# Transposing seven of ten probability blocks of each attention head with VectorE and DMA in place of TensorE

## The reference, cut to what matters

```python
q = jnp.einsum('bpd,hde->bphe', x, W_Q) + b_Q        # k, v likewise
scores = jnp.einsum('bqhe,bkhe->bhqk', q, k) / ATTN_SCALE
scores = jnp.where(causal, scores, IGNORE)
attn = jax.nn.softmax(scores, axis=-1)
z = jnp.einsum('bkhe,bhqk->bqhe', v, attn)
out = jnp.einsum('bqhe,hed->bqd', z, W_O) + b_O
```

## Time and profile before

| | |
|---|---|
| median of 3 runs | 533.88 us |
| the profiled execution | 534.24 us |
| its span | 532.4 us |
| TensorE (PE) busy | 514.5 us, 97% |
| weight loads (PEld) | 464.4 us, 87% |
| VectorE (DVE) | 385.2 us, 72% |
| ScalarE (ACT) | 292.8 us, 55% |
| GpSimd (POOL) | 191.9 us, 36% |
| mean granted TensorE clock | 0.989 of full |

### The profile page before, as it was taken

How to read it: one execution, slowest core, us unless ns; L and a number is a source line. 1 busy time by engine, 2 the same in 40 slices (tenths; PEclk the granted TensorE clock), 3 DMA queues, 4 the chain that set the end, 5 groups by cost and what they waited for, 6 DMA issues and landing times.

```text
span 532.4 us, 9326 instructions
## 1 busy us (share of the span) xinstructions
PE 514.5 (97%) x3302; PEld 464.4 (87%) x3302; DVE 385.2 (72%) x970; ACT 292.8 (55%) x688; POOL 191.9 (36%) x277
## 2 busy tenths in 40 slices
PE   8999999999999899999999999999999999999972
PEld 7888889898888789999999999999998999999861
DVE  2757876855555978768668668777777787667897
ACT  2446533564545565655656656566566565665552
POOL 2236142434656335214223223322512543222234
PEclk9999999999999999999999999999999999999995
DMA  9900000000000021000200200200200200000002
GB/s 281 356 6 1 1 0 1 2 1 1 2 0 1 0 81 46 36 1 1 80 1 1 81 2 1 79 2 2 80 0 2 80 2 0 2 1 0 2 2 79
DMA packets 8333, 17.52 MB, mean 33 GB/s; under 512 B 480, under 2 KB 6752, under 8 KB 7264
## 3 DMA queue, kind: packets, MB, share of 16 engines
q1 hardware_dynamic: 7200, 15.89, 8.7%
q10 hardware_dynamic: 1088, 1.05, 0.6%
HBM read 15.88 MB, written 1.05 MB: 32 GB/s over the span
## 4 chain that ended last, share of the span: by engine, by line
PE 86%; DVE 7%; ACT 2%; DMA 2%; issue 1%; POOL 1%; SPq 0%; DVEq 0%; ACTq 0%
PE bank L303 20%; PE bank L305 20%; PE bank L304 20%; PE bank L559 6%; PE bank L550 4%; PE bank L549 4%; PE bank L551 4%; PE bank L488 3%; PE bank L487 3%; DMA Wv_sb<-wv 2%; PE bank L498 1%; PE bank L500 1%; DVE XN L1021 1%; DVE SM L1291 1%; PE bank L354 1%
## 5 line engine op out<-in xcount | busy, mean ns | idle before, releaser
L797 ACT ACTIVATE PR<-SM,nmax 128x128 f32<-128x128 f32 (+3 forms) x128 | 71.9, 562 | 100.7 <-DVE nmax L1291 100.5
L1291 DVE CUSTOM_DVE_ANT_0 SM<-bank,causal 128x128 f32<-128x128 f32 (+3 forms) x128 | 60.7, 484 | 18.4 <-PE bank L551 18.3
L962 POOL TENSOR_TENSOR PR<-PR,rec 128x128 f32<-128x128 f32 x32 | 12.8, 400 | 140.2 <-DVE rec L1298 140.2
L1302 DVE TENSOR_TENSOR PT_lo<-bank,PT_hi 128x128 fp32r<-128x128 f32 (+3 forms) x128 | 59.3, 485 | 2.1 <-ACT PT_hi L802 0.3
L802 ACT CAST PT_hi<-bank 128x128 fp32r<-128x128 f32 (+3 forms) x128 | 50.0, 423 | 5.1 <-PE bank L559 4.3
L303 PE MATMUL bank<-XT_hi,W_hi 128*128 128x512 f32 x128 | 50.6, 395 | 0.2 <-DVE XT_lo L1029 0.2
L918 POOL TENSOR_TENSOR E_lo<-E,E_hi 128x512 fp32r<-128x512 f32 x24 | 31.0, 1297 | 54.6 <-ACT E_hi L721 47.6
L305 PE MATMUL bank<-XT_hi,W_lo 128*128 128x512 f32 x128 | 50.5, 395 | 0.0
L304 PE MATMUL bank<-XT_lo,W_hi 128*128 128x512 f32 x128 | 50.4, 394 | 0.0
L559 PE MATMUL bank<-ident,PR 128*128 128x128 f32 x320 | 46.2, 273 | 1.8 <-DVE PT_lo L1302 0.8
L549 PE MATMUL bank<-K_hi,Q_hi 128*128 128x256 f32 (+2 forms) x128 | 46.5, 364 | 0.0
(11 more groups left out here) (174 smaller groups left out, 1621.9 us busy)
## 6 DMA issues: line engine op xcount, KB each, us to landing
stage<-pack SPq DMA_DIRECT2D x8, 1027.0 KB, 4.9
X<-x SPq DMA_DIRECT2D x2, 512.0 KB, 8.8
wraw<-wupT SPq DMA_DIRECT2D x1, 1024.0 KB, 10.1
wraw<-wgateT SPq DMA_DIRECT2D x1, 1024.0 KB, 12.0
wraw<-wdownT SPq DMA_DIRECT2D x1, 1024.0 KB, 15.8
Wq_sb<-wq ACTq DMA_DIRECT2D x3, 256.0 KB, 5.3
Wk_sb<-wk SPq DMA_DIRECT2D x3, 256.0 KB, 4.7
Wv_sb<-wv SPq DMA_DIRECT2D x3, 256.0 KB, 8.4
```

Source lines behind the costliest of these rows:

```text
L797: act.activation(PR[:, c, 0:(c + 1) * P], SM[:, c % 2, 0:(c + 1) * P], ACT.Exp, bias=nmax1[:, c:c + 1], scale=-1.0, accum_out=sum1[:, c:c ...
L1291: dve.tensor_tensor_reduce(SM[:, c % 2, 0:n], bank[2 + c % 2][:, 0:n], causal[:, SEQ - n:SEQ], 1.0, HIGHEST, ALU.add, ALU.min, nmax1[:, c: ...
L1302: dve.tensor_tensor(PT_lo[w % 2][:, 0:c + 1, c * P:(c + 1) * P], bank[4 + c % 2][:, 0:(c + 1) * P].rearrange("p (j q) -> p j q", q=P), PT_ ...
```

## The change

For windows 1 to 25 only T0 and T1 stay on TensorE. T2 and T3 (seven blocks) go another way:

- DVE transposes row blocks 2 and 3 of PR, in SBUF, in blocks of 32x32 into `BT` (`U2` at the end of the window before, `U3` early in the head's window). What is left is to exchange the 32-partition strips.
- SyncE issues 12 DMAs, one for each pair of different strips: 32 partitions x 8 runs of 128 B, 32 KB each, from `BT` to `MV`. The four strips that stay in their partitions are copied by ACT (`D0` to `D3`, 32 partitions x 256 elements each).
- One window later ACT rounds MV to PT_hi (`C2`, `C3`), POOL (not DVE) writes PT_lo (`moved_low`), and PE does the product with V (`B0`) near the window's end, after S3.
- Output projections are spread, one part in each window, a head pair later; Z_hi and Z_lo exist twice.
- The refills of `stage` are issued by ACT, no longer by SyncE.
- The 256-column minimum is gone: row block 0 of the scores and the last key block of the product with V stream 128 columns, everywhere. With it go six memsets (four on POOL, two on DVE); two memsets of BT on POOL are new.
- Windows 27 to 31 keep their lists; 0, 1 and 26 have lists of transition.

The diff, cut to its core:

```diff
+QUAD = P // 4
+MOVES = 16 * 12
...
+        memb = ExitStack()
+        BT = [sb(f"BT{i}", [P, CT, 2, P], F32, memb) for i in range(2)]
+        MV = [sb(f"MV{i}", [P, CT, 2, P], F32, memb) for i in range(2)]
...
+        FIRST_MOVED, LAST_MOVED = 1, WINDOWS - 7
+        STEADY_PE = (steps("T0 T1 S0 O0 S1 Q0 S2 K1 S3 B0 V2"), steps("T0 T1 S0 Q0 S1 O0 S2 K1 S3 B0 V2"))
+        STEADY_ACT = (steps("W2 T0 T1 S0 C2 C3 S1 Q0 D0 D1 S2 D2 D3 K1 B0 S3"),
+                      steps("W2 T0 T1 S0 Q0 C2 C3 S1 D0 D1 S2 D2 D3 K1 B0 S3"))
+        STEADY_DVE = (steps("S0 W2 U3 T0 T1 O0 S1 Q0 S2 R0 K1 S3 B0 R1 U2"),
+                      steps("S0 W2 U3 T0 T1 S1 Q0 O0 S2 R0 K1 S3 B0 R1 U2"))
...
+            0: steps("T0 T1 S0 T2 T3 S1 Q0 S2 K1 A0 S3 V2"),
+            1: steps("T0 T1 S0 S1 Q0 S2 K1 S3 V2"),
+            WINDOWS - 6: steps("T0 T1 S0 O0 S1 T2 T3 Q0 S2 K1 B0 S3 V2 A0"),
+            WINDOWS - 5: EVEN_PE,
...
+        def by_dma(w):
+
+            return FIRST_MOVED <= w <= LAST_MOVED
+
+        def moved_windows(w):
+
+            return max(0, min(w, LAST_MOVED + 1) - FIRST_MOVED)
+
+        def turns(w):
+
+            return CT * w - 2 * moved_windows(w)
...
+            return (w - 3) // 2 if w % 2 else (w - 4) // 2, 1 - w % 2
...
-            for p in range(1, PAIRS):
-
-                sp.wait_ge(wb_dve, p)
-                sp.wait_ge(wb_pool, p)
-                sp.dma_start(stage[:], pack1[p]).then_inc(ld_pack, 16)
+            sp.wait_ge(bt_zero, 1)
+            for w in range(FIRST_MOVED, LAST_MOVED + 1):
+                sp.wait_ge(bt_done, 2 * moved_windows(w + 1))
+                if w >= FIRST_MOVED + 2:
+                    sp.wait_ge(mv_lo, 2 * moved_windows(w - 1))
+                for j in range(CT):
+                    for i in range(CT):
+                        if i == j:
+                            continue
+                        sp.dma_start(MV[w % 2][j * QUAD:(j + 1) * QUAD, :, :, i * QUAD:(i + 1) * QUAD],
+                                     BT[w % 2][i * QUAD:(i + 1) * QUAD, :, :, j * QUAD:(j + 1) * QUAD]
+                                     ).then_inc(moved[w % 2], 16)
...
-                n = max((c + 1) * P, 2 * P)
+                n = (c + 1) * P
...
-                pe.wait_ge(t_free, 4 * w + c + 1)
+                if w > 0 or c > 1:
+                    pe.wait_ge(t_free, turns(w) + c - 1)
...
-                pe.wait_ge(t_free, 4 * w + 6)
+                pe.wait_ge(t_free, turns(w + 1))
+                if by_dma(w):
+                    pe.wait_ge(mv_lo, 2 * moved_windows(w + 1))
                 pe.wait_ge(z_free, w + 1)
                 if h == 0:
                     pe.wait_ge(pj_lo, 6 * (g + 1))
-                if w == 1:
-                    pe.wait_ge(pt_zero, 1)
                 for j in range(CT):
-                    q0 = min(j * P, SEQ - 2 * P)
+                    q0 = j * P
...
+                    cols = slice(max(2 * r, j) * P, 2 * (r + 1) * P)
...
+            def move_diagonal(w, i):
+
+                if i == 0:
+                    act.wait_ge(bt_done, 2 * moved_windows(w + 1))
+                    if w >= FIRST_MOVED + 2:
+                        act.wait_ge(mv_lo, 2 * moved_windows(w - 1))
+                part = (slice(i * QUAD, (i + 1) * QUAD), slice(None), slice(None), slice(i * QUAD, (i + 1) * QUAD))
+                act.copy(MV[w % 2][part], BT[w % 2][part]).then_inc(mv_diag, 1)
+
+            def moved_hi(w, c):
+                if c == 2:
+                    act.wait_ge(moved[w % 2], MOVES * ((w - FIRST_MOVED) // 2 + 1))
+                    act.wait_ge(mv_diag, CT * moved_windows(w + 1))
+                act.copy(PT_hi[w % 2][:, 0:c + 1, c * P:(c + 1) * P], MV[w % 2][:, 0:c + 1, c - 2, :]).then_inc(mv_hi, 1)
...
+            def refill(p):
+
+                act.wait_ge(wb_dve, p)
+                act.wait_ge(wb_pool, p)
+                act.dma_start(stage[:], pack1[p]).then_inc(ld_pack, 16)
...
+                        if w > 0 and stage_refill(w - 1):
+                            refill(stage_refill(w - 1))
...
+            def moved_low(w):
+
+                for c in range(2, CT):
+                    pool.wait_ge(mv_hi, 2 * moved_windows(w) + c - 1)
+                    pool.tensor_tensor(PT_lo[w % 2][:, 0:c + 1, c * P:(c + 1) * P], MV[w % 2][:, 0:c + 1, c - 2, :],
+                                       PT_hi[w % 2][:, 0:c + 1, c * P:(c + 1) * P], ALU.subtract).then_inc(mv_lo, 1)
...
+            pool.wait_ge(down_done, FFN_STEPS)
+            for turned in BT:
+                last = pool.memset(turned[:, CT - 1, 0, :], 0.0)
+            last.then_inc(bt_zero, 1)
...
+            def turn_blocks(w, c):
+                dve.wait_ge(p_norm, 4 * w + c + 1)
+                if c == 2:
+                    dve.wait_ge(bt_zero, 1)
+                    if w >= FIRST_MOVED + 2:
+                        dve.wait_ge(moved[w % 2], MOVES * ((w - FIRST_MOVED) // 2))
+                        dve.wait_ge(mv_diag, CT * moved_windows(w - 1))
+                dve.transpose(BT[w % 2][:, 0:c + 1, c - 2, :],
+                              PR[:, c, 0:(c + 1) * P].rearrange("p (j q) -> p j q", q=P)).then_inc(bt_done, 1)
```

More of the change, by code:

```diff
@@ L148, in build @@
         PT_lo = [sb(f"PT_lo{i}", [P, CT, SEQ], F32R) for i in range(2)]
-        Z_hi = sb("Z_hi", [P, 2, SEQ], F32R)
-        Z_lo = sb("Z_lo", [P, 2, SEQ], F32R)
+        memf = ExitStack()
+        SIL = sb("SIL", [P, 3, SEQ], F32, memf)
+        HID = sb("HID", [P, 3, SEQ], F32, memf)
+        HID_hi = sb("HID_hi", [P, 3, SEQ], F32R, memf)
+        HID_lo = sb("HID_lo", [P, 3, SEQ], F32R, memf)
+        memf.close()
+        Z_hi = [sb(f"Z_hi{i}", [P, 2, SEQ], F32R) for i in range(2)]
+        Z_lo = [sb(f"Z_lo{i}", [P, 2, SEQ], F32R) for i in range(2)]
         nmax1 = sb("nmax1", [P, CT])
@@ L206, in build @@
         s_psum, s_max, s_exp, s_rec, p_norm = (sem(n) for n in ("s_psum", "s_max", "s_exp", "s_rec", "p_norm"))
-        t_psum, pt_hi, t_free, pt_zero = sem("t_psum"), sem("pt_hi"), sem("t_free"), sem("pt_zero")
+        t_psum, pt_hi, t_free = sem("t_psum"), sem("pt_hi"), sem("t_free")
+        bt_zero, bt_done = sem("bt_zero"), sem("bt_done")
+        moved = [sem(f"moved{i}") for i in range(2)]
+        mv_diag, mv_hi, mv_lo = sem("mv_diag"), sem("mv_hi"), sem("mv_lo")
         z_psum, z_hi, z_free = sem("z_psum"), sem("z_hi"), sem("z_free")
@@ new lines, in build @@
+        ACT_ORDER = {w: STEADY_ACT[w % 2] for w in range(2, LAST_MOVED + 1)} | {
+            0: EVEN_ACT,
+            1: steps("W2 T0 T1 S0 S1 Q0 D0 D1 S2 D2 D3 K1 S3"),
+            WINDOWS - 6: steps("W2 T0 T1 S0 C2 C3 S1 T2 Q0 S2 T3 K1 B0 S3 A0"),
+            WINDOWS - 5: EVEN_ACT,
+            WINDOWS - 4: EVEN_ACT,
+            WINDOWS - 3: ODD_ACT,
+            WINDOWS - 2: steps("T0 T1 S0 S1 T2 S2 T3 W2 S3"),
+            WINDOWS - 1: steps("T0 T1 B0 T2 A0 T3 A1 X0 I0 I1")}
+        DVE_ORDER = {w: STEADY_DVE[w % 2] for w in range(2, LAST_MOVED)} | {
+            0: steps("T0 T1 S0 W2 T2 T3 S1 Q0 S2 R0 K1 S3 A0 R1 U2"),
+            1: steps("S0 W2 U3 T0 T1 S1 Q0 S2 R0 K1 S3 R1 U2"),
+            LAST_MOVED: steps("S0 W2 U3 T0 T1 S1 Q0 O0 S2 R0 K1 S3 B0 R1"),
+            WINDOWS - 6: steps("S0 W2 T0 T1 O0 S1 T2 Q0 S2 T3 R0 K1 B0 S3 R1 A0"),
+            WINDOWS - 5: EVEN_DVE,
+            WINDOWS - 4: steps("T0 T1 S0 W2 O0 T2 T3 S1 L0 Q0 S2 O1 L1 R0 K1 S3 A0 R1 L2"),
+            WINDOWS - 3: steps("T0 T1 S0 W2 N0 Q0 T2 T3 S1 N1 S2 R0 K1 N2 S3 A0 R1 N3"),
+            WINDOWS - 2: steps("T0 T1 S0 S1 X0 S2 T2 R0 T3 W2 S3 O0 R1 X1 X2 O1"),
+            WINDOWS - 1: steps("T0 T1 B0 T2 A0 T3 X3 O0")}
@@ L812, in z_high_half @@
                 p, b, h = place(WINDOWS - 1)
+                g = WINDOWS // 2 - 1
                 cols = slice(2 * r * P, 2 * (r + 1) * P)
                 act.wait_ge(z_psum, WINDOWS + r)
-                act.activation(Z_hi[:, h, cols], bank[2 + r][:, cols], ACT.Identity, bias=bv[p % 2][:, h:h + 1],
+                act.activation(Z_hi[g % 2][:, h, cols], bank[2 + r][:, cols], ACT.Identity, bias=bv[p % 2][:, h:h + 1],
                                scale=1.0).then_inc(z_hi, 1)
@@ L858, in window @@
                         z_high(w)
+                    elif kind == "C":
+                        moved_hi(w - 1, c)
+                    elif kind == "D":
+                        move_diagonal(w, c)
                     elif kind == "A":
@@ L936, in split_b @@
                                    WO_hi[p % 2][:].rearrange("p h o -> p (h o)"), ALU.subtract).then_inc(wb_pool, 1)
-            pool.wait_ge(o0_psum, 2)
-            for turned in (PT_hi[1], PT_lo[1]):
-                pool.memset(turned[:, CT - 1, 2 * P:3 * P].bitcast(F32), 0.0)
-                last = pool.memset(turned[:, 1, 0:P].bitcast(F32), 0.0)
-            last.then_inc(pt_zero, 1)
             for q in range(FFN_STEPS):
@@ L1300, in probs_lo @@
             def probs_lo(w, c):
-                dve.wait_ge(pt_hi, 4 * w + c + 1)
```

(7 more changed lines are left out.)

79 lines of the change are left out of this document (39 added, 40 removed).

## The result

The changed kernel takes **538.16 us** (median of 4 runs, 537.88 to 538.73), the kernel before beside it on the same chip 533.91 us (533.76 to 534.23). The ratio is **1.008, 95% interval 1.0063 to 1.0098**: 0.8% slower, where the forecast was 517.2 us, 3% faster. It lies above the range of 505 to 531 and on the other side of no change.

What follows compares the result with a forecast made beforehand. PE was taken to bound the kernel (97% busy, no gap in the changed windows). In profiled time 534.24 - 19.25 - 1.4 + 1.5 + 2.5 = 517.6, hence a forecast of 517.2 us, range 505 to 531.

Steps and rivals of the forecast that it cites:

- Removed, and narrower matmuls (1, 2): On PE: 175 transposes gone, 19.25 us less; 195 matmuls of 128 instead of 256 columns, 1.4 us less.
- the rival of 10.3 us more: On PE: 128-column matmuls cost 0.057 us each, not 0.11, so another 10.3 us go, 506.9 us; chance 0.15.
- VectorE (3): Two PT_lo evacuations leave, two SBUF turns come at 1.0 us a window; 7.7 of 9.7 us busy, nothing on the path.
- ScalarE (4): Four new diagonal copies, 1.5 us a window, take ACT from 6.4 to 7.9 of 9.7 us; hidden.
- GpSimd (5): Two more subtractions take POOL from 3.5 to 5.8 us a window; hidden.
- SyncE and the transfers (6, 7): Twelve DMAs a window at 0.45 us each plus 2.2 to land, 7.6 us; 9 ns per 128 B run.
- the 0.72 that I allowed: Microseconds per strip DMA before C2 comes too late for PE, from a detour allowance of 10.9 us less 2.2 over 12.
- that rival: SyncE's loop of 12 issues becomes the bound from 0.88 us per DMA, near 556 or 650 us; chance 0.11.
- The late detour: ACT's wait for moved strips holds up the window, above 0.72 us per DMA or behind a refill; about 528 us; chance 0.17.
- The start (8): Windows 1 and 2: 2.5 us of idle PE, between 0 and 5.
- the 1.5 charged: Microseconds added in all for refills sharing the DMA engines with seven of the detours.
- a wait takes up all 19 us: No gain though PE does less, because a wait absorbs the removed transposes' time; chance 0.02.

Runs made afterwards that it cites:

- the stripped kernel: The changed kernel without weight preparation for pairs 1 to 7, and with strip transfers and diagonal copies in windows 1 and 2 only: 519.83 us.
- the kernel with four moves: The changed kernel with D2, D3 behind K1, K and V casts behind odd window's reciprocals, V bias copied by ScalarE, pair 1's refill in window 0: 527.77 us.
- the refill's new place: The refill issued behind C3 instead of behind W2, added to the kernel with four moves: 521.75 us, ratio 0.9769 against the kernel before.

## Why the prediction was wrong

*Removed, and narrower matmuls (1, 2): right.* L631 has 145 transposes where L559 had 320, as said. The windows of after that no weight preparation touches take 9.77 us at the least, as the stripped kernel's do; forecast 9.7. The narrow matmuls give 1 us (forecast 1.4) and start 0.11 to 0.12 apart; the rival of 10.3 us more falls.

*VectorE (3): size too low, harmless.* The two turns in 32x32 blocks (busy us, mean ns):

```profile
L1421 DVE STREAM_TRANSPOSE BT<-PR 128x512 f32<-128x512 f32 x25 | 17.5, 701 | 0.0
L1421 DVE STREAM_TRANSPOSE BT<-PR 128x384 f32<-128x384 f32 x25 | 14.5, 579 | 0.7 <-issue 0.4
```

1.28 us, not 1.0, as much as the evacuations that they replace.

*ScalarE (4): size right, "hidden" wrong. This is the step that failed.* ACT's busy time is 195.79 us in 25 windows, 7.8 each (forecast 7.9), a diagonal copy 0.40 us. But I put busy time against the length of the window, 7.9 of 9.7, and took the difference for slack. The four copies stand in a chain that goes from ScalarE to VectorE and back, and that chain's length, not the engine's load, was what had to fit. Their place alone is worth 11 us. I had named the order of the steps on ScalarE for C2, and never asked what D2 and D3 stand in front of.

*GpSimd (5): size right (141.70/25 = 5.7 us, forecast 5.8), "hidden" wrong again.* The casts of weights were absent from my sum although the change moves them: the K cast went behind U3, next to GpSimd's longer list. And the longer list costs VectorE time. DVE lines of the kernel after (ns min/median/max), then of before:

```profile
L1332 DVE CAST W_hi<-stage x8: 1128/1143/1499, 138.7 to 438.4; 128x512 fp32r<-128x512 f32 x8
L1336 DVE COPY bv<-stage x8: 164/1286/1295, 188.2 to 459.4; 128x2 f32<-128x2 f32 x8
```
```profile
L1222 DVE CAST W_hi<-stage x8: 417/827/839, 138.6 to 437.7; 128x512 fp32r<-128x512 f32 x8
L1226 DVE COPY bv<-stage x8: 159/159/165, 187.8 to 443.5; 128x2 f32<-128x2 f32 x8
```

1.4 us more per pair. With the casts moved away from GpSimd's subtractions the V cast takes 0.41 us.

*SyncE and the transfers (6, 7): too cheap.* Issues are 0.65 us apart (0.61 the issue itself), forecast 0.45; the last lands 2.0 us later. That is 11 x 0.65 + 2.0 = 9.2 us for the detour, forecast 7.6, and 9.1 to 10.6 are measured (median 9.7), since most rows of twelve have a slow issue:

```profile
L403 SPq DMA_DIRECT2D MV<-BT x300: 585/611/1862, 196.7 to 458.0; - x150
```

The 0.65 are below the 0.72 that I allowed, so SyncE is no bound (that rival falls; the 2.0 us to landing do overlap from DMA to DMA; the Trainium skill has the fixed 2.0 us that I quoted under "Anatomy of one DMA — SWDGE (gpsimd) path" of "DMA: Bandwidth & Descriptors", not under "Measured"). But of the 10.9 us that I allowed for the detour the measured 9.1 to 10.6 leave 0.3 to 1.8, and C2 waited 4.7 and 3.4 us where a refill was in the way. A run of 128 B costs 13.5 ns, not 9: q1's time grows from 741 to 1432 us of engine time (8.7% and 16.7% of 16 spans), although the refills' 344 us went over to q10; (1432 - 397)/76,800. A refill takes 344/7/16 = 3.1 us of all 16 engines. The late detour, a rival at 0.17, is real. In after it was worth 4.2 us, and there it came from rows of issues that start late and have a slow issue in them, not from refills. "A refill delays the moves" became true only with the order mended: windows 3 and 7 of the kernel with four moves are 10 us too long together, and the refill's new place gave back 6.0. I had set the refill against the moves of its own window; what it met were the last ones of the window before.

*The start (8): 5.3 us of idle PE in windows 1 and 2, counted from start to start, forecast 2.5,* a little over my bound of 5. 2.3 of them are one wait for GpSimd's split: the refill for pair 1 goes out at 194.2 in window 1 where SyncE sent it at 189.7.

The balance in profiled spans: forecast -16.6, measured +3.7, so 20.3 missing. Windows 3 to 25 take 241.5 us where 23 x 9.77 are 224.7: 16.8, less the 1.5 charged, is 15.3. The start is 2.8. The windows' own 9.77 instead of 9.69 (10.51 less 0.77 and 1.4/29) is 1.8 in 23 windows. That makes 19.9. The side on which it ended had 0.13 in my numbers, for SyncE and for "a wait takes up all 19 us". The second came true, and I dismissed it with "spare time of 20% or more on each other engine", the same mistake as in step 4; ScalarE's 1.8 of 9.7 us are not even 20%. (One sum of the rivals is off: 25 x 0.9 + 2.5 on top of 534 is 559, not 556. Nothing hangs on it.)

## What to carry to other kernels

When a kernel has an order written out by hand, spare busy time on an engine does not hide new work. Take the shortest chain that crosses engines within one period (here maximum, exponential, K_hi, K_lo, maximum), see how early its last link ends before the engine that bounds needs it, and place new work behind the steps that others wait for, never ahead. Look at the fullest period, not the mean one: here two of four windows carried the next weights, and the second of them and the one behind it lost 11 of the 16.8 us. When one wait is healed, read the next trace for what comes into step: shorter windows brought refill and strips together, and only then was the refill's place worth 6 us. And when a row of small DMAs must be in time, count its slowest case, not its median.
